# Low rows of the query stacks: a matmul into PSUM and a second ScalarE copy instead of a VectorE step

## What is computed

```python
x = x + tanh(g_xattn[L]) * attention_L(layernorm(x), ctx)
x = x + tanh(g_ffn[L])   * experts_L(layernorm(x))
```

```python
q = heads(x @ wq + bq); k = heads(ctx @ wk + bk); v = heads(ctx @ wv + bv)
attn = softmax(q @ k.T * scale)        # layer 2: banded, no biases; layer 3: masked scores are -10000
out  = (attn @ v) @ wo + bo
```

## Time and profile before

| | |
|---|---|
| time, median of 3 runs | 682.08 us (681.06 to 682.86) |
| time of the profiled execution | 681.47 us |
| its span, first to last instruction | 679.7 us |
| TensorE matmul busy | 622.9 us, 92% |
| VectorE busy | 506.3 us, 74% |
| ScalarE busy | 368.4 us, 54% |
| mean granted TensorE clock | 0.975 |

### The profile page before, as it was taken

The page is one execution under the profiler, slowest core; times in us unless marked ns, Lnnn a source line. Parts: engine busy times, 40 slices in busy tenths (PEclk is TensorE's granted clock), DMA queues, the critical chain, the costliest instruction groups (busy, mean ns, idle before and its releaser), DMA issues.

```text
span 679.7 us, 11675 instructions
## 1 busy us (share of the span) xinstructions
PE 622.9 (92%) x3531; PEld 437.2 (64%) x3555; DVE 506.3 (74%) x1287; ACT 368.4 (54%) x635; POOL 229.9 (34%) x438
## 2 busy tenths in 40 slices
PE   9898999888999799988997899999987999969996
PEld 6684777556776467745665467777665777645774
DVE  6868988879773488878535798888769888457886
ACT  6346554435667255425662477777642665624774
POOL 3212466331103026621121166766620000202672
PEclk9989999989999989999999899999998999998999
DMA  8254111010000001110002011111000000000111
GB/s 275 74 156 132 48 47 35 19 41 3 27 3 4 24 0 47 36 32 2 5 5 69 1 40 40 39 39 46 22 26 3 6 24 3 2 1 6 43 39 40
DMA packets 22446, 25.51 MB, mean 38 GB/s; under 512 B 4930, under 2 KB 19938, under 8 KB 22396
## 3 DMA queue, kind: packets, MB, share of 16 engines
q1 hardware_dynamic: 21820, 23.87, 12.0%
q10 hardware_dynamic: 576, 1.02, 0.4%
HBM read 20.58 MB, written 3.77 MB: 36 GB/s over the span
## 4 chain that ended last, share of the span: by engine, by line
PE 76%; DVE 14%; ACT 4%; issue 3%; DMA 1%; POOL 1%; DVEq 0%; SPq 0%; ACTq 0%
PE PS L673 13%; PE PS L675 12%; PE PS L674 12%; PE PS L695 5%; PE PS L905 5%; PE PS L813 4%; PE PS L516 4%; PE PS L888 4%; DVE negmax L1581 2%; PE PS L920 2%; DVE qst L1541 2%; DVE consts L1587 2%; PE PS L885 1%; PE PS L861 1%; ACT pT L1186 1%
## 5 line engine op out<-in xcount | busy, mean ns | idle before, releaser
L419 POOL TENSOR_TENSOR wpair<-ring,ones_col 128x128 fp32r<-128x128 f32 (+1 forms) x150 | 79.7, 531 | 160.2 <-PE PS L675 113.9
L1486 DVE TENSOR_TENSOR pT<-pT,PS 128x512 f32<-128x512 f32 x150 | 102.5, 684 | 28.7 <-ACT pT L1087 23.2
L1186 ACT ACTIVATE pT<-PS 128x512 f32<-128x512 f32 x160 | 92.0, 592 | 50.2 <-PE PS L888 40.9
L1492 DVE TENSOR_TENSOR hid_lo<-pT,hid_hi 128x512 fp32r<-128x512 f32 x150 | 108.5, 723 | 2.9 <-ACT hid_hi L1094 1.6
L1094 ACT ACTIVATE hid_hi<-pT 128x512 fp32r<-128x512 f32 x150 | 93.8, 625 | 22.7 <-DVE pT L1486 22.3
L421 POOL TENSOR_TENSOR wpair<-ring,wpair 128x128 fp32r<-128x128 f32 (+1 forms) x150 | 100.9, 673 | 11.7
L673 PE MATMUL PS<-hid_hi,wpair 128*128 128x512 f32 x150 | 85.9, 573 | 4.4 <-DVE hid_lo L1492 4.4
L673 PE MATMUL PS<-xhi,wpair 128*128 128x512 f32 x204 | 84.7, 415 | 2.1 <-DVE pT L1486 1.4
L1087 ACT ACTIVATE pT<-PS,ring 128x512 f32<-128x512 f32 x96 | 65.8, 688 | 36.7 <-PE PS L675 36.7
L675 PE MATMUL PS<-xhi,wpair 128*128 128x512 f32 x204 | 82.5, 404 | 0.0
L674 PE MATMUL PS<-xlo,wpair 128*128 128x512 f32 x204 | 82.3, 404 | 0.0
(11 more groups left out here) (233 smaller groups left out, 1129.1 us busy)
## 6 DMA issues: line engine op xcount, KB each, us to landing
ring<-in_mlp SPq DMA_DIRECT2D x48, 128.5 KB, 2.0
ring<-in_glu SPq DMA_DIRECT2D x27, 192.0 KB, 2.4
kz<-keys SPq DMA_DIRECT2D x36, 96.0 KB
keys<-qst SPq DMA_DIRECT2D x6, 512.0 KB, 3.6
qst<-kfull SPq DMA_DIRECT2D x96, 4.0 KB
wq<-in_wq SPq DMA_DIRECT2D x3, 256.0 KB, 3.6
x_res<-in_x SPq DMA_DIRECT2D x1, 512.0 KB, 4.8
ctx_tok<-in_ctx_tok SPq DMA_DIRECT2D x1, 512.0 KB, 6.2
```

What stands on the lines that cost most here:

```text
L419: pool.tensor_tensor(wpair[:, pair, 0, c], w, ones, ALU.mult).then_inc(M["wstep"], 1)
L1186: act.activation(pT[:, w % 8, :], PS[:, 2 + w % 2, :], ACT.Exp, scale=sc).then_inc(A["p"], 1)
L1486: dve.tensor_tensor(hid[:, hf, :], src[:, hf, :], PS[:, 6 + hf, :], ALU.mult).then_inc(M["hid"], 1)
L1492: dve.tensor_tensor(hid_lo[:, kept, :], hid[:, kept % 2, :], hid_hi[:, kept, :].bitcast(f32), ALU.subtract).then_inc(M["lo"], 1)
```

## The change

VectorE's `finish_queries` is removed. In its place TensorE multiplies the stack that ScalarE has just written by a constant matrix `third` (one on the diagonal in the third group of rows, zero elsewhere) and adds it to the bank that still holds q (`low_queries`). The third group of the bank then holds q minus its high part and the other groups still q. ScalarE copies the whole bank to the stack a second time, without a factor (`finish_queries` on ScalarE). `third` is made once by a VectorE instruction at the start. In layer 2 the projections move from p = 2, 3, 5, 6 to 2, 3, 6, 7.

```diff
-        Q_AT = (4, 5, 8, 9)
+        Q_AT, R_AT = (4, 5, 8, 9), (6, 7, 10, 11)
+        QW_AT, RW_AT = (2, 3, 6, 7), (4, 5, 8, 9)
...
+                def low_queries(hf, a, bank):
+
+                    pe.wait_ge(A["qt"], pre["qt"] + HGRP * hf + a + 1)
+                    pe.matmul(PS[:, bank, :], third[:, :], queries(L, hf, a), start=False, stop=True,
+                              skip_group_check=True).then_inc(A["qr"], 1)
+
                 layer_norm(2 * L, (0,))
+                if L == 1:
+                    pe.wait_ge(set_dve, 4)
...
                 for a in range(HGRP):
                     project_queries(0, a, 2 + a)
+                    if a > 0:
+                        low_queries(0, a - 1, 1 + a)
+                low_queries(0, HGRP - 1, 1 + HGRP)
                 layer_norm(2 * L, (1,))
...
                         if p in Q_AT:
                             project_queries(1, Q_AT.index(p), 4 + Q_AT.index(p) % 2)
+                        if p in R_AT:
+                            low_queries(1, R_AT.index(p), 4 + R_AT.index(p) % 2)
...
-                        if p in (2, 3, 5, 6):
-                            a = (2, 3, 5, 6).index(p)
-                            project_queries(1, a, 4 + a % 2)
+                        if p in QW_AT:
+                            project_queries(1, QW_AT.index(p), 4 + QW_AT.index(p) % 2)
+                        if p in RW_AT:
+                            low_queries(1, RW_AT.index(p), 4 + RW_AT.index(p) % 2)
...
+                def finish_queries(hf, a, bank):
+
+                    act.wait_ge(A["qr"], pre["qr"] + HGRP * hf + a + 1)
+                    act.activation(queries(L, hf, a), PS[:, bank, :], ACT.Copy).then_inc(A["qe"], 1)
+
                 layer_norm(2 * L, (0,))
                 for a in range(HGRP):
                     take_queries(0, a, 2 + a)
+                    if a > 0:
+                        finish_queries(0, a - 1, 1 + a)
+                finish_queries(0, HGRP - 1, 1 + HGRP)
                 layer_norm(2 * L, (1,))
                 act.activation(warm[:, :], gates[:, 0:1], ACT.Exp).then_inc(astep, 1)
                 def loop():
-                    for a in range(HGRP):
-                        take_queries(1, a, 4 + a % 2)
-                        if a % 2 == 1:
-                            copy_max(a // 2)
+                    for pair in range(2):
+                        for a in (2 * pair, 2 * pair + 1):
+                            take_queries(1, a, 4 + a % 2)
+                        finish_queries(1, 2 * pair, 4)
+                        copy_max(pair)
+                        finish_queries(1, 2 * pair + 1, 5)
...
                 def window_loop():
-                    for a in range(HGRP):
-                        take_queries(1, a, 4 + a % 2)
-                        if a % 2 == 1:
-                            copy_max(a // 2)
-                    copy_max(2)
+                    for pair in range(2):
+                        take_queries(1, 2 * pair, 4)
+                        if pair == 1:
+                            copy_max(1)
+                        take_queries(1, 2 * pair + 1, 5)
+                        finish_queries(1, 2 * pair, 4)
+                        copy_max(2 * pair)
+                        finish_queries(1, 2 * pair + 1, 5)
...
                 dve.tensor_copy(pick[:, :], consts[0:PARTS * EP, C_ID3:C_ID3 + EP]).then_inc(set_dve, 1)
+                dve.tensor_scalar(third[:, :], ident, consts[:, C_SGN + 1:C_SGN + 2], None, ALU.mult).then_inc(set_dve, 1)
...
-                def finish_queries(hf, a, bank):
-
-                    dst = queries(L, hf, a)
-                    dve.wait_ge(A["qt"], pre["qt"] + HGRP * hf + a + 1)
-                    dve.scalar_tensor_tensor(out=dst, in0=PS[:, bank, :], scalar=consts[:, C_SGN + 1:C_SGN + 2],
-                                             in1=dst.bitcast(f32), op0=ALU.mult, op1=ALU.add).then_inc(A["qe"], 1)
-
-                for a in range(HGRP):
-                    finish_queries(0, a, 2 + a)
                 ln_turned(2 * L, (1,))
...
-                    if v in (3, 4, 6, 7):
-                        a = (3, 4, 6, 7).index(v)
-                        finish_queries(1, a, 4 + a % 2)
...
-                    if v in (5, 6, 9, 10):
-                        a = (5, 6, 9, 10).index(v)
-                        finish_queries(1, a, 4 + a % 2)
```

More of the change, by code:

```diff
@@ L110, in build @@
         ones2 = sb("ones2", [P, HALF], f32r)
-        minus = sb("minus", [P, P], f32r)
+        minus, third = sb("minus", [P, P], f32r), sb("third", [P, P], f32r)
         bo = {L: sb(f"bo{L}", [P, P]) for L in (1, 3)}
@@ L215, in build @@
                                           "exp", "mix", "mo", "moe", "z", "ze", "vo", "voe", "out")}
-        adds = dict(q=8, qt=8, qe=8, s=B * H, mx=B * H, nmp=4 * B, nmt=4 * B, nmc=4 * B,
+        adds = dict(q=8, qt=8, qr=8, qe=8, s=B * H, mx=B * H, nmp=4 * B, nmt=4 * B, nmc=4 * B,
                     st=B * H, p=B * H, pv=4 * B, oe=B, ot=TB * B, on=TB * B, fin_t=2, fin_e=2, fin=2)
```

## The result

| | before | changed |
|---|---|---|
| time, median | 682.73 us (19 runs, 679.08 to 685.0) | 684.48 us (19 runs, 682.78 to 688.4) |
| ratio to before | | 1.0036, 95% interval 1.002 to 1.0052 |
| profiled execution, its span | 681.47, 679.7 us | 683.82, 682.0 us |
| mean granted TensorE clock of it | 0.975 | 0.978 |

The change makes the kernel slower by 1.75 us (medians) to 2.5 us (ratio). The forecast was 683.4, that is +1.3, with a range of 681.0 to 685.8. Over all timed executions with a clock on record the kernel before takes 682.65 us in the mean, at a mean granted clock of 0.9739 (62 executions; one of 3354 us, in the slow state, is left out), and the changed kernel 685.08 us at 0.9741 (29 executions).

What follows compares the result with a forecast made beforehand. TensorE, busy 92%, was taken to bound the kernel, with VectorE on 14% of the chain. Fronts +5.47, ramps -3.10 and clock -1.05 gave +1.3 us on a median of 682.08: 683.4 us, range 681.0 to 685.8.

Steps and rivals of the forecast that it cites:

- Front: Start of each attention block, up to the second half's `xlo`: ScalarE's doubled copies delay `xlo`, +5.47 us over three layers.
- back to back: Fronts: after the second first-copy, ScalarE's remaining copies were taken to follow one another without gaps in layer 1.
- pace of 0.667 us: Fronts: start-to-start time of ScalarE's copy with a factor, read from layer 2's timeline; also the new copy's upper bound.
- take 3: Layer 1's front: ScalarE's last first-copy of a stack, forecast to start at 148.75 us, its matmul at 149.47.
- Ramp: Row maxima, from the first reduction on: VectorE's relief pays only in part, -3.10 us; bounds 0 and -7.9.
- Rival C: Ramps pay in full as scores don't wait for projections: 681.1 us, or 679 with copies partly hidden; under 680.03, chance 0.08.
- The clock: Layer 3's ramp: a fall of TensorE's clock goes away, -1.05 us; bounds 0 and -1.4.
- this dip: Late in layer 3's ramp, TensorE's granted clock at 0.57 over 522 to 526 us, estimated to cost 1.05 us.
- rival B: TensorE's clock falls at the fronts' new gaps, or layer 3's fall stays: 684.4 us, 685.5 with one more; chance 0.30.

Runs made afterwards that it cites:

- e1: Changed kernel with the first half of the tokens finished by VectorE as before, the second half by matmul and ScalarE copy; 679.19 us, 0.9945 of before.
- e3: Changed kernel with TensorE's turning of the second half and ScalarE's `xhi` moved ahead of the last two finishing copies; 679.62 us, 0.9963 of before.
- e5: Changed kernel with a per-partition factor of one on the 24 finishing copies, to make each dearer; 685.70 us, 1.0034 of before.
- e6: Kernel before without the second half's finishing step and nothing in its place, so its results differ; 679.16 us, 0.9944 of before.
- e7: Changed kernel run once more, unedited, for its clock; 685.34 us, 1.0037 of before.
- e2: Changed kernel with the second half finished by VectorE inside the loop as before, the first half by matmul and ScalarE copy; 690.81 us, 1.0123 of before.
- e8: e3 with the first two scores (layer 2: one) ahead of TensorE's turning and VectorE's first reductions ahead of `xlo`; 678.44 us, 0.9947 of before.
- e9: Kernel before run once more, unedited, for its clock in layer 3; 679.33 us in one execution.

## Why the prediction was right, and where a term was off

*Front, predicted +5.47 (1.66, 2.16, 1.65): measured +1.57, +1.95, +1.57, in all +5.09.* The mechanism is shown by e1 (it goes when the front goes back) and e3 (it shrinks by 1.2 per layer when `xhi`, with the turning that feeds it, is moved). What was wrong is the picture of ScalarE "back to back": e5 shows a relay with TensorE, in which the copy's own length hardly counts. The pace of 0.667 us was misread as well. In the rows it came from, the copies wait for TensorE's projections, whose last matmuls start every 0.69 us:

```profile
307.41 0.39 PE L787 MATMUL PS<-xhi,wqpair 128*128 128x512 f32 x1
...
308.10 0.39 PE L787 MATMUL PS<-xhi,wqpair 128*128 128x512 f32 x1
...
308.79 0.39 PE L787 MATMUL PS<-xhi,wqpair 128*128 128x512 f32 x1
```

Only the last of the four is left at ScalarE's own pace, 0.59 us. With ScalarE's own paces (0.59 with a factor, 0.48 to 0.50 without) take 3 of layer 1 would start 2.1 to 2.2 us behind take 1; predicted were 2.48, measured 2.43. Copies priced too dear stood in for waits that the sum did not have, so that the front came out this near is luck in part.

*Ramp, predicted -3.10 (-0.88, -0.12, -2.10): measured with the clock up -0.80, -0.17, -1.87, in all -2.84.* That a layer's four removed steps don't pay in full is shown by e6: with nothing in their place the ramp is still 9.24 us in layer 1 and 10.17 in layer 3, and the waits for scores behind projections are in its trace. Rival C, the ramp paid in full, falls with it.

*Without the clock* the terms make +2.37 predicted and +2.25 measured.

*The clock, predicted -1.05: this is the term that was mis-sized.* It said "I take this dip away". The late fall does go in all three traces of the change, and is worth 1.1 to 1.2 us (8.40 to 8.50 against 7.29). But in two of three the clock falls at the start of the same ramp instead, which costs 11.73 - 10.19 = 1.54 us. Over three traces that is about -1.2 + 1.0 = -0.2. The timed executions say the same of the kernel as a whole: the mean clock is 0.9739 before and 0.9741 changed, that is 35.7 and 35.5 us at 1.2 GHz, a difference of 0.2 with an interval of 1.8 either way. At 0.39 us each that is -0.1, 0.7 either way. So the clock gives back nothing that can be told from none, and the +2.25 of the fronts and ramps is near the whole difference of the means, 685.08 - 682.65 = +2.4. This is rival B in part: its mechanism happened, in layer 3 only, and the time lies between the forecast and B's 685.5. The passage of the Trainium skill cited there ("TensorE: Matmul & The Clock Gate", What's actually happening) had it that idling brings the clock down. In these traces the early fall comes behind TensorE's waits of 0.54 and 1.35 us, but the same waits in e7 and e2 brought none; that one leads to the other is not shown.

*Outside the changed stages* the prediction had no term. In the three traces of before, the stretch from layer 2's first weighing to layer 3's first projection took 176.05, 176.00 and 176.27 us, in the three of the change 177.35, 178.51 and 177.98, with a longer fall of the clock near 375 to 385 us. No work was added there, and the length does not go with the work of the change: e6, which only takes work away, has 178.40 there, and e8 175.78. The first stretch, up to layer 1's first projection, took 141.5 to 145.7 us over the same six traces. It goes with the clock and not with the kernel: 6.8 us at 1.2 GHz in the two shortest, 13.7 in the next two, 17.1 in the two longest. Whether stages that end elsewhere shift the fall near 375 us for good, or three traces are too few, stays open; if they do, the mean clocks say that it is made up for elsewhere.

## What to carry to other kernels

Moving a step to an emptier engine moves it into that engine's order: look at what stands next in the queue that takes it (here `xhi`, on which the relieved engine itself was waiting), and move that ahead of the step. Price a removed step by what the engine would wait for next, and measure that bound with a kernel that leaves the step out. Split a change by place before judging it: one half of this one gains 0.55% by itself, and the other loses 1.2% by itself (0.75% by its fronts, the rest at a lower clock).

## What was not expected of the hardware

The granted clock is the main difference found between executions of one program here: fronts and ramps repeat to 0.1 us, while each of the 14 traces has five to nine falls to 1.2 GHz whose places partly wander. In one of the three of before (e9) a fall at 159.5 us made layer 1 from n11 to the weighing 6.34 us long, against 5.33. The 19 timed executions of the change show it too: the five at a mean clock of 0.978 took 682.78 to 683.82 us, the two at 0.969 took 688.1 and 688.4.

When two ScalarE copies of 128x512 stand in a row and the second has nothing to wait for, it starts about 0.10 us before the first ends, whichever kinds they are: a copy with a per-partition factor (0.69 us) is left after 0.59 us, for a copy without a factor in the changed kernel and for one with it in e5; one without a factor (0.59 us) after 0.48 to 0.50.
